# A state-space layer with a quantized feed-forward block: who prepares the feed-forward weights, and in what order the first tokens run

## The reference, cut to what matters

```python
zxbcdt = u @ W_in                                  # 256 -> 1288
z, xBC, dt = split(zxbcdt)                         # 512, 768, 8
xBC = silu(causal_conv(xBC, 4 taps))               # x: 512, B: 128, C: 128
dt = softplus(dt + dt_bias);  A = -exp(A_log)      # 8 heads of 64
y = ssd(x * dt, A * dt, B, C) + x * D              # scan, written as masked products
y = y * silu(z);  y = y * rsqrt(mean(y**2) + EPS) * norm_scale
h = layernorm(u + y @ W_out)
# gate, up: 256 -> 2048, down: 2048 -> 256; two 4-bit codes a byte, one scale for 32 values
W = LUT[codes] * scales
out = layernorm(h + (gelu(h @ Wg) * (h @ Wu)) @ Wd)
```

## Time and profile before

| | |
|---|---|
| median of 3 runs | 956.05 us (955.52 to 957.06) |
| profiled execution | 955.01 us |
| its span, first to last instruction | 953.3 us |
| TensorE busy | 892.7 us, 94% |
| VectorE busy | 704.9 us, 74% |
| ScalarE busy | 532.2 us, 56% |
| GpSimd busy | 72.3 us, 8% |
| mean granted TensorE clock | 0.971 of full speed |

### The profile page before, as it was taken

How to read it: one execution, slowest core, us unless ns; L and a number is a source line. 1 busy time by engine, 2 the same in 40 slices (tenths; PEclk the granted TensorE clock), 3 DMA queues, 4 the chain that set the end, 5 groups by cost and what they waited for, 6 DMA issues and landing times.

```text
span 953.3 us, 16507 instructions
## 1 busy us (share of the span) xinstructions
PE 892.7 (94%) x5632; PEld 773.0 (81%) x5632; DVE 704.9 (74%) x1566; ACT 532.2 (56%) x1016; POOL 72.3 (8%) x104
## 2 busy tenths in 40 slices
PE   4777789899999999999999999999999999999997
PEld 3446678788898888888888888888888888888887
DVE  6767988787769776786779876786779776867453
ACT  4743486448645775448735674547635674456232
POOL 2101000200011000200020000200020000200000
PEclk9787899999999999999999999999999999999999
DMA  4111100010002000010001000010002000100010
GB/s 135 33 58 49 32 18 12 23 45 1 1 23 67 0 0 22 22 44 0 0 22 66 0 0 22 31 35 0 0 22 67 1 1 13 45 12 1 1 35 12
DMA packets 18651, 23.13 MB, mean 24 GB/s; under 512 B 1584, under 2 KB 15152, under 8 KB 18608
## 3 DMA queue, kind: packets, MB, share of 16 engines
q1 hardware_dynamic: 18176, 22.56, 7.4%
q10 hardware_dynamic: 432, 0.03, 0.0%
HBM read 14.19 MB, written 4.19 MB: 19 GB/s over the span
## 4 chain that ended last, share of the span: by engine, by line
PE 78%; DVE 10%; issue 6%; POOL 3%; ACT 2%; DMA 1%; POOLq 0%; DVEq 0%; SPq 0%; ACTq 0%
PE gate_bank L493 6%; PE up_bank L493 6%; PE up_bank L495 6%; PE up_bank L494 6%; PE gate_bank L495 5%; PE gate_bank L494 5%; PE down L493 5%; PE down L495 5%; PE mixer L493 5%; PE down L494 5%; PE mixer L495 5%; PE mixer L494 5%; PE mixer L573 3%; DVE xbc L904 2%; PE mixer L552 2%
## 5 line engine op out<-in xcount | busy, mean ns | idle before, releaser
L493 PE MATMUL down<-wd_hi,in_hi 128*128 128x256 f32 x512 | 145.1, 283 | 0.7 <-DVE in_lo L1035 0.7
L495 PE MATMUL down<-wd_hi,in_lo 128*128 128x256 f32 x512 | 144.0, 281 | 0.0
L494 PE MATMUL down<-wd_lo,in_hi 128*128 128x256 f32 x512 | 143.8, 281 | 0.0
L904 DVE SCALAR_TENSOR_TENSOR xbc<-mixer,chan,xbc 128x510 f32<-128x510 f32 (+1 forms) x162 | 110.9, 685 | 27.8 <-ACT xbc L703 26.1
L760 ACT ACTIVATE in_hi<-act_sb 128x512 fp32r<-128x512 f32 (+1 forms) x144 | 83.4, 579 | 65.3 <-PE down L495 53.7
L1049 DVE SCALAR_TENSOR_TENSOR act_sb<-up_bank,act_sb 128x512 f32<-128x512 f32 (+1 forms) x144 | 90.4, 628 | 37.5 <-PE up_bank L495 18.5
L774 ACT ACTIVATE act_sb<-gate_bank 128x512 f32<-128x512 f32 (+1 forms) x144 | 79.0, 548 | 67.7 <-PE gate_bank L495 67.0
L493 PE MATMUL gate_bank<-hT_hi,wg_hi 128*128 128x512 f32 (+1 forms) x288 | 111.4, 387 | 3.1 <-DVE wg_lo L1102 3.1
L493 PE MATMUL up_bank<-hT_hi,wu_hi 128*128 128x512 f32 (+1 forms) x288 | 108.4, 376 | 6.4 <-DVE act_sb L1049 6.4
L495 PE MATMUL up_bank<-hT_hi,wu_lo 128*128 128x512 f32 (+1 forms) x288 | 107.8, 374 | 0.0
L494 PE MATMUL up_bank<-hT_lo,wu_hi 128*128 128x512 f32 (+1 forms) x288 | 107.8, 374 | 0.0
(11 more groups left out here) (200 smaller groups left out, 1936.2 us busy)
## 6 DMA issues: line engine op xcount, KB each, us to landing
xbc<-in_u_t_dram SPq DMA_DIRECT2D x7, 512.0 KB, 3.6
h_sb<-in_u_dram SPq DMA_DIRECT2D x7, 512.0 KB, 3.8
h_res<-h_sb SPq DMA_DIRECT2D x7, 512.0 KB, 2.9
out_dram<-h_res SPq DMA_DIRECT2D x7, 512.0 KB, 2.9
scales<-in_ffn_s_dram SPq DMA_DIRECT2D x24, 128.0 KB, 2.1
packed<-in_ffn_w_dram SPq DMA_DIRECT2D x8, 96.0 KB, 2.1
xbc<-in_u_t_dram SPq DMA_DIRECT2D x2, 256.0 KB, 2.8
xbc<-in_W_in_dram SPq DMA_DIRECT2D x1, 512.0 KB, 6.2
```

Of the source, the lines that this page charges most:

```text
L493: nc.tensor.matmul(dst, lh, rh, start=first, stop=False, skip_group_check=True)
L494: nc.tensor.matmul(dst, lh, rl, start=False, stop=False, skip_group_check=True)
L495: return nc.tensor.matmul(dst, ll, rh, start=False, stop=last, skip_group_check=True)
L904: ins = stt(acc[:, :, d:], src[:, :, 0:SEQ - d], chan[:, c:c + 1], acc[:, :, d:], ALU.mult, ALU.add)
```

## The change

`BESIDE_FIRST` falls from 12 to 9: nine chunks are prepared beside group -1 and fifteen beside group 0. All 24 lower parts are made by VectorE; the 36 products of TensorE and the twelve copies of ScalarE for them go. The five dictionaries become two, and one VectorE step does everything for its chunk. Group -1 gets another order: no chunk ahead of the first projection, `CB0` behind `x0`, `R0` and `R1` early (R1 in a buffer of its own), both decay weights (`W0`, `W1`) behind both `D`. The projections of group 0's `uT`, `dt` and `x4` come ahead of group -1's `F1`. On the queue the B and C columns of `W_in` go ahead of the first codes, and group 0's input is loaded at chunk 8 instead of 14. `W` is a step of its own in all groups, right behind `D`, so full groups keep their order.

```diff
-    "first": ["dt", "x4", "x5", "x0", "x1", "z0", "x2", "z1", "x3", "z2", "z3", "CB0", "D0a", "D0b", "XT0",
+    "first": ["dt", "x4", "x5", "x0", "CB0", "x1", "z0", "x2", "z1", "x3", "z2", "z3", "D0a", "D0b", "XT0",
...
-    "first": [["x5", "x0", "x1", "z0", "x2", "z1", "x3", "z2", "z3", "CB0", "R0", "D0", "R1", "XT0", "D1", "Y0",
-               "XT1", "Y1", "g0", "S0", "op0", "g1", "S1", "op1", "ln1", "ln2"], []],
+    "first": [["x5", "x0", "CB0", "x1", "R0", "z0", "x2", "z1", "R1", "x3", "z2", "z3", "D0", "XT0", "D1", "W0", "W1",
+               "Y0", "XT1", "g0", "Y1", "S0", "op0", "g1", "S1", "uT", "op1", "ln1", "ln2"], []],
...
+BESIDE_FIRST = 9
+WEIGHT_STEPS = {FIRST: {"x4": 0, "x1": 1, "z3": 2, "D0": 3, "W1": 4, "g0": 5, "Y1": 6, "g1": 7, "ln1": 8},
+                0: {"x5": 9, "z0": 10, "z1": 11, 2: 12, 3: 13, 4: 14, "XT0": 15, "W0": 16, 6: 17, "XT1": 18, 7: 19,
+                    "W1": 20, 8: 21, "XT2": 22, 9: 23, 10: 24, 11: 25}}
+UPPER = {FIRST: {"x5": 0, "z0": 1, "XT0": 2, "D1": 3, "Y0": 4, "Y1": 5, "g1": 6, "S1": 7, "ln2": 8},
+         0: {0: 9, 1: 10, 2: 11, "x2": 12, "x3": 13, "CB0": 14, 5: 15, 6: 16, "Y0": 17, 7: 18, "D1": 19, 8: 20,
+             "R2": 21, 9: 22, "D2": 23}}
...
             sp.dma_start(u32[:, :, 0:HALF], uT_of(FIRST)).then_inc(uT_in.sem, 16)
+            sp.dma_start(bc_raw, win_v[:, :, B0:NIN]).then_inc(bc_in.sem, 16)
             load_block(0)
-            sp.dma_start(bc_raw, win_v[:, :, B0:NIN]).then_inc(bc_in.sem, 16)
+            sp.dma_start(x_raw, win_v[:, :, X0:B0]).then_inc(x_in.sem, 16)
             load_scales(0)
-            sp.dma_start(x_raw, win_v[:, :, X0:B0]).then_inc(x_in.sem, 16)
-            load_block(1)
             load_scales(1)
             sp.dma_start(z_raw, win_v[:, :, 0:X0]).then_inc(z_in.sem, 16)
+            load_block(1)
...
             for c in range(2, CHUNKS):
+                if c == BESIDE_FIRST - 1:
+                    load_uT(0)
                 if c == BESIDE_FIRST + 2:
-                    load_uT(0)
-
-                    sp.wait_ge(wt_lo.sem, BESIDE_FIRST)
+
+                    sp.wait_ge(wt_lo.sem, BESIDE_FIRST - 1)
...
+            def weight_step(c):
+                if c % 3 == 0 and c < CHUNKS:
+                    decode(c // 3)
+                if c >= 2:
+                    rest(c - 2)
+                if c < CHUNKS:
+                    value(c)
```

More of the change, by code:

```diff
@@ L38 @@
 SLOTS = {
[3 rows of a table removed]
[3 rows of a table added]
              ["S3", "op3", "ln1"], ["ln2"]],
[4 rows of a table removed]
[L53 to L68, removed]
[4 rows of a table added]
+             [], [], []]}
+BESIDE_FIRST = 9
[5 more added lines that the diff above has]
+             "R2": 21, 9: 22, "D2": 23}}
 def kind_of(g):
@@ L220, in mamba_ffn_kernel, with R_of @@
         wout_raw = zs[:, :, HALF:]
[L222 removed]
+        R_first = [[x.rearrange("p k (h l) -> p (k h) l", l=P) for x in pair]
+                   for pair in ((hT_hi[:, :, :], hT_lo[:, :, :]), (wd_hi[:, 12:16, :], wd_lo[:, 12:16, :]))]
         dec_first = act_sb[:, :, :].rearrange("p k (h l) -> p (k h) l", l=P)
[L224 to L227 removed]
+        def R_of(g, i):
+            return R_first[i] if kind_of(g) == "first" else (R_hi, R_lo)
         def dec_of(g, i):
@@ L331, in wait_R @@
         def wait_R(eng, i, g):
[L333 to L336, removed]
+            if kind_of(g) != "first":
+                wait_ready(eng, f"D{i - 1}b" if i % 2 else f"E{i // 2 - 1}" if i else "z3", g)
             wait(eng, dA_ok, g, 1)
@@ L362, in run @@
             last = kind_of(g) == "last"
-            if not last:
+            if not first and not last:
                 mixer("uT", g + 1)
+            if first:
+                mixer("dt", g + 1)
+                mixer("x4", g + 1)
             ffn("F1", 0, g)
@@ L368, in run @@
                 ffn("final_sum", 0, g - 1)
-            if not last:
+            if not first and not last:
                 mixer("dt", g + 1)
                 mixer("x4", g + 1)
-                if not first:
-                    ffn("final_norm", 0, g - 1)
+                ffn("final_norm", 0, g - 1)
         def run_end(ffn):
@@ L550, in mixer @@
                         hs = slice(4 * n, 4 * n + 4)
-                        upper, lower = R_of(g)
+                        upper, lower = R_of(g, i)
                         nc.tensor.matmul(bank(g, use)[:, :], after_r[:, :], upper[:, hs, :], start=True, stop=False)
@@ L560, in mixer @@
                         for a, rows in ((1, P), (0, HP)):
-                            for n, part in enumerate(R_of(g)):
+                            for n, part in enumerate(R_of(g, i)):
                                 mm = nc.tensor.matmul(bank(g, use)[0:rows, :],
@@ L646, in ffn @@
                     down(n, f)
[L648 to L658, removed]
             def any_mixer(name, g):
@@ L781, in upper @@
                 nc.scalar.activation(prep_dst(c)[0], chunk_out(c), ACT.Copy).then_inc(wt_hi.sem, 1)
[L783 to L786, removed]
             def prep(g, item):
[L789 to L792, removed]
+                if item in UPPER[g]:
+                    upper(UPPER[g][item])
             def any_mixer(name, g):
                 mixer(name, g)
+                if name == "x5" and kind_of(g) == "first":
+                    act.wait_ge(z_in.sem, 16)
+                    nc.scalar.activation(win_hi[:, :, 0:X0], z_raw, ACT.Copy).then_inc(win_top.sem, 1)
                 if name == "x1" and kind_of(g) == "first":
@@ L808, in _ @@
             act.wait_ge(consts.sem, 5)
-            nc.scalar.activation(minus_i, ident[:, :], ACT.Copy, scale=-1.0).then_inc(crt.sem, 1)
             mixer("uT", FIRST)
@@ L941, in mixer @@
                        dt_sb[:, i, :].unsqueeze(2).to_broadcast([P, H, HP]), ALU.mult).then_inc(x_ok.sem, 1)
-                    if kind_of(g) == "first" and i == 0:
-                        x_tail(i, g)
-                elif kind == "D":
+                elif kind == "W":
                     d = dec_of(g, i)
@@ L1098, in rest @@
                 dve.wait_ge(wt_hi.sem, c + 1)
-                dve.wait_ge(wt_lo.sem, c)
                 upper, lower = prep_dst(c)
                 tt(lower, chunk_out(c), f32(upper), ALU.subtract).then_inc(wt_lo.sem, 1)
-            def prep(g, item):
-                for c in LOWER[g].get(item, ()) if kind_of(g) != "first" else ():
-                    rest(c)
-                for c in VALUE[g].get(item, ()):
-                    value(c)
-                for b in DECODE[g].get(item, ()):
-                    decode(b)
+            def weight_step(c):
[5 more added lines that the diff above has]
+                    value(c)
+            def prep(g, item):
+                if item in WEIGHT_STEPS[g]:
+                    weight_step(WEIGHT_STEPS[g][item])
             dve.wait_ge(consts.sem, 5)
@@ L1118, in _ @@
             ts(chan[:, 0:30], chan[:, 0:30], 0.5, None, ALU.mult).then_inc(crt.sem, 1)
-            decode(0)
-            value(0)
-            value(1)
             dve.wait_ge(win_top.sem, 1)
```

44 lines of the change are left out of this document (18 added, 26 removed), and 10 rows, old and new, of the table SLOTS.

## The result

The changed kernel takes 977.92 us (median of 4 runs, 977.44 to 978.16) against 955.78 (4 runs, 955.40 to 957.06): ratio 1.0229, 95% interval 1.0211 to 1.0246. It is slower by 22 us, where 10 were forecast and 971 was the upper end. Its profiled execution took 978.16 us, its span is 976.4 us, the mean granted clock 0.953 instead of 0.971.

A forecast was written before the change was run, and what follows sets the result against it. VectorE was taken to set the pace ahead of 179 us, TensorE after. -0.2 - 2.7 + 7.6 + 7.7 - 1.0 = +11.4, less 1 us: +10.4 on the profiled 955.0, 965.4; as a median 966, range 957 to 971.

The forecast's parts named there:

- Part 1: The start: TensorE's first product at about 8.0 us, taps of x4 at 11.95 instead of 15.36: -3.4 us.
- Part 3: From op1 to x5 of group 0: x4 starts 2.8 us behind op1, x5 comes 12.4 us behind op1: -2.7 us.
- Part 4: Scales queued behind codes: six VectorE waits of 1.9 us at steps 3 to 18, four in group 0: +7.6 us.
- Rival (b): Group -1 closes its waits, only the two scale waits left: another -8.3 us, 957.5; chance 0.14.
- (c): Group 0 paced by the chain over ScalarE and TensorE, hiding VectorE's added 15.3 us: 953; chance 0.10.
- (e): Scales land in time because SyncE gets ahead somewhere, 11.4 us fall away: 954.6, no difference; chance 0.03.
- part 5: Group 0: VectorE's added values, rests and decodes cost +7.7 us; last steps and late exps net -1.0 us.
- Net -1.0 us: Group 0: last steps partly fill later waits, against late exps of +1.5, -0.7, +1.1; bounds +3 to -7.
- the filling: Group 0: VectorE's last steps, 23 to 25, 2.4 us, lie among the later waits and partly fill them.
- Part 2: Group -1 up to op1: VectorE's work +2.6 us, idle -0.4; op1 taken at 69.0 us: -0.2 us.
- I take 1 us off: The sum: step-by-step counts find new waits more readily than cover for them, so +11.4 became +10.4 us.
- Rival (d): TensorE stays at 1.2 GHz; added stalls pull group 0's clock from 0.90 to 0.75: 970; chance 0.11.

The follow-up runs named there:

- the scales first: The changed kernel with one edit in the transfer queue, scales 3k issued ahead of packed block k + 1: 966.74 us, ratio 1.0114.
- both together: The changed kernel with scales ahead of codes, value ahead of rest, and six upper parts of group 0 behind their convolution or exp: 955.36 us, ratio 0.9999.
- both orders: The changed kernel with scales ahead of codes, and each VectorE step's value ahead of the rest, which comes one step earlier: 957.57 us, ratio 1.0020.
- uppers later: The changed kernel with scales ahead of codes, and group 0's fifteen upper parts on ScalarE behind the convolution or exp they preceded: 958.71 us, ratio 1.0027.
- `x4` without products: The kernel before with group -1's lower parts by VectorE, no products for them, and group 0's x4 ahead of F1: 960.35 us, ratio 1.0035.

## Why the prediction was right in direction and wrong in size

**Right.** Part 1: 3.6 us for 3.4. Part 3: 2.4 for 2.7, with two misses that nearly cancel: `x4` starts 2.1 us behind `op1` instead of 2.8, and takes 6.0 us instead of 5.6, all at half clock. Part 4: six waits at the steps named, by the mechanism named, 13.3 us for 11.4 (2.1 to 2.4 each); moving the scales gave 11.2 back. The added work, nearly: group 0's VectorE is busy 9.2 us more for 7.7, and the lower parts alone cost 6.6 us. Nothing changes behind group 0's `F1`. Rival (b) is out, group -1's idle time grew; so are (c) and (e). (By its own terms (b) would come to 966 - 8.3 = 957.7, not 957.5.)

**The step that failed** is in part 5: "Net -1.0 us". It said that beyond the scales, group 0's waits would shrink by 1 us. They grew: group 0's idle time rose by 12.9 us, of which 8.5 are scales; the other 4.4 stand where -1.0 was written, and VectorE's busy time there is 1.5 us above the count. (The terms named don't give -1.0 either: +1.5 - 0.7 + 1.1 = +1.9 for the exps, and 2.4 us of work can fill 2.4 at most, so -0.5.) The late exps, put at +1.9, cost nothing on top: VectorE waits 4.4 us for them in group 0, 4.6 before. The error is the filling, for the new work filled nothing and made new waits. Waits for the convolution rose from 0.8 to 2.4 us, those for `in_hi` and for `y` came anew, 1.2 us, and idle times too short for the list rose from 0.5 to 2.1, such as the 0.14 us of a value behind its rest (98.79 to 98.93).

What the count had not followed step by step is a chain: a value waits for its own rest, ScalarE's upper part waits for the value, the convolution or exp stands behind the upper part, and VectorE waits for that, six times in group 0, 6.8 us; with the upper parts moved one wait of 0.7 us is left. Cutting it at ScalarE gave 8.0 us with the scales first and 7.4 without; cutting it inside VectorE's step gave 9.2; both together 11.4. That is more than the 4.4 us, as the edits also close waits that the kernel before has.

**Part 2** was short as well: `op1` at 72.5, not 69.0, and so past the 72 that the prediction had named as a sign of being wrong. The work was 1.3 us more than counted (45.2 - 41.4 = 3.9 for 2.6). Idle time rose by 3.0 us where -0.4 was written; the two waits for scales are 4.7 us of the idle time, where 3.8 had been counted, so 2.5 us of other waits were missed. The long ones named were there (2.1 us for `CB0`, 1.9 for `z0`). Together these are 4.7 us (1.3 of work, 0.9 at the scales, 2.5 of other waits); taking 69.0 instead of 68.0 had covered 1.0 of them, which leaves 3.7.

**"I take 1 us off"**, because a count finds new waits more readily than cover for them, had the wrong sign: this count missed waits. The misses add up: 3.7 before `op1`, 0.3 and -0.2, 7.9 in group 0 and this 1 us make 12.7. The forecast rose by 10.4 on the profiled execution, which rose by 23.2.

**Products and clock.** They were counted at nothing on the path. For the kernel as changed that nearly held: giving `x4` full clock by 50 products gave nothing net, as these took 3 us longer than the gap they were to fill. With 60 products ahead of `S1`, `op1`'s own ran at full clock and it started at 71.92 instead of 72.47 us: 0.5 us. Around `x4` the traces of the kernel before put the price of their absence at 1.8 us between `op1` and `x5`; the medians would have 5.7 (8.3 - 2.6), and the rest isn't located. The lower parts ahead of `op1` cost 6.1 us with `x4` moved (69.33 to 75.48) and 7.4 without. The Trainium skill, TensorE: Matmul & The Clock Gate, "What's actually happening", calls the throttled state the default and lets activity release it. The traces agree in part: in `x4` right behind the products the clock is 1.00, without them 0.50; in the kernel before `x4` starts 4.6 us behind their end, and the stretch from 75 us on is at 0.53. Rival (d) put the clock's loss in group 0. It did fall there, to 0.82, and was 0.92 again without the scales' waits; these gave back 11.2 us for their 13.3, so no price of the clock is seen on top of them.

**What stays open.** In three kernels (both orders; uppers later; `x4` without products) single executions spread over 6 to 8 us, some in two clusters (956.2 to 956.7 and 961.5 to 961.8 for the uppers), without a cause that was looked for. Their differences of 1 to 2 us are not to be read. One trace says where: the profiled execution of the uppers kernel, 961.52 us, is of the upper cluster. From 178 to 200 us its TensorE clock is 0.58 and then 0.82, where the kernel with the scales first has 0.86 and 1.00 in the same places ahead of and behind `F1`, and from `F1` of group 0 to the end it takes 778.8 us instead of 774.6. Why the clock is lower in one execution than in another isn't shown. The changed kernel with the 36 products kept was not run, nor the start's VectorE time beside GpSimd by itself.

## What to carry to other kernels

When several pieces of work become one step, write down what each piece waits for inside the step, and what stands behind each on its in-order engine: here undoing each of a queue issue behind the decode, a value behind its rest and an upper part ahead of the convolution gave 8 to 11 us, as much as the added work in group 0 (9.2). Put on a shared engine first what the pacing engine needs, then what only prepares. Before work is taken from TensorE, see at which clock the block behind it runs: `dt` and `x4` took 3.2 us right behind it and 6.0 without it, of which 1.8 reached the pacing engine in the traces. The move of `x4` alone, on the kernel before, is the version to keep. And look at which of a kernel's executions was profiled before a median is explained by its trace: here a middle one and the profiled one were 3.5 us apart.

## What the runs showed of the hardware

- How long TensorE had just been idle did not tell at which clock the next block ran. With 60 products ahead of `S1` the clock was 1.00 and fell while `op1`'s own products ran, behind idle times of 0.94 us and less (0.28 us for a product, then 0.37 and 0.42); it was 0.50 in the 3.7 us of idle behind them and in `x4`. Before the change, 69 to 75 us stood at 1.00 with 1.9 us of busy TensorE and 4.1 us of idle in one piece, and 75 to 80.5 us, `x4`, at 0.53 with no idle. With the 50 products it was 0.50 in `op1` and 0.98 in the first 1.9 us of the products right behind.
- The same `dt` and `x4` took 3.2 us at clock 1.00 (2.4 GHz) and 6.0 at 0.50 (1.2 GHz).
- A VectorE instruction that overwrites what the one before it reads, with a semaphore between the two, starts 0.2 us later than one that doesn't wait (0.82 us behind the start of the one before for 0.61).
